# Weight sums moved into the quantisation loop, a deferred tail in the down projection, and a bf16 intermediate, in an eight-core two-layer transformer kernel

## The reference

```python
def _weight_quant(w):
    scale = 1.0 / jnp.clip(jnp.mean(jnp.abs(w)), 1e-05)
    return jnp.clip(jnp.round(w * scale), -1.0, 1.0) / scale
def _act_quant(x):
    scale = 127.0 / jnp.clip(jnp.max(jnp.abs(x), axis=-1, keepdims=True), 1e-05)
    return jnp.clip(jnp.round(x * scale), -128.0, 127.0) / scale
def _bitlinear(x, w):
    return jnp.einsum('bsi,oi->bso', _act_quant(x), _weight_quant(w))
gate = jax.nn.silu(_bitlinear(x, w_gate))      # w_gate, w_up: 4096 x 1024
up = _bitlinear(x, w_up)
out = _bitlinear(gate * up, w_down)            # w_down: 1024 x 4096
```

## Time and profile before

| | us |
|---|---|
| timed runs, median of 2 | 10397.83 (10381.49 to 10414.16) |
| the profiled execution, device time | 10226.14 |
| its span, slowest core (core 3) | 10224.6 |
| spans of the 8 cores | 10200.0 to 10224.6 |
| mean granted TensorE clock of the 8 cores | 0.623 to 0.624 of full speed |

### The profile page before, as it was taken

One profiled execution on the slowest core, in us unless ns is written; L12 is line 12 of the kernel. 1 busy time (PEld: TensorE's weight loads), 2 busy tenths in 40 slices (PEclk: granted clock), 3 DMA queues, 4 the chain that ended last, 5 costly groups with the idle time before them and its releaser, 6 DMA issues.

```text
span 10224.6 us, 48395 instructions; the slowest of 8 cores (10200.0 to 10224.6 us)
## 1 busy us (share of the span) xinstructions
PE 3471.7 (34%) x13683; PEld 1368.5 (13%) x13683; DVE 6251.7 (61%) x4796; ACT 1875.6 (18%) x2102; POOL 0.2 (0%) x4
## 2 busy tenths in 40 slices
PE   5766645999812111111011111000056531212112
PEld 2211112333301000000000000000023210101001
DVE  2555542222224999997899999966733325565565
ACT  0233311111111222222222222110121111111111
POOL 0000000000000000000000000000000000000000
PEclk9655557999955555555555565555578765555555
DMA  2000012111143332233323323234022221100100
GB/s 85 5 0 0 0 58 81 66 58 58 44 156 111 88 89 80 85 90 89 92 89 88 89 80 88 82 126 144 23 80 77 84 70 39 36 26 25 37 25 27
DMA packets 237113, 682.50 MB, mean 67 GB/s; under 512 B 31291, under 2 KB 64300, under 8 KB 230516
## 3 DMA queue, kind: packets, MB, share of 16 engines
q1 hardware_dynamic: 236852, 679.41, 21.3%
HBM read 599.36 MB, written 79.95 MB: 66 GB/s over the span
## 4 chain that ended last, share of the span: by engine, by line
DVE 48%; PE 26%; issue 10%; DMA 8%; ACT 6%; SPq 1%; DVEq 1%; ACTq 0%
DVE b_sl L1174 12%; DVE b_sl L1187 6%; DVE b_sl L1162 6%; DVE qd2B L1405 5%; PE p_hB L670 4%; PE p_eoB L701 4%; DVE ternB L1401 3%; PE p_dnB L1737 3%; PE p_gA L1556 2%; PE p_uA L1561 2%; DVE rb L443 2%; ACT attbuf L438 2%; DVE zbuf L432 2%; DVE qdD L1405 1%; DMA wstgB<-W 1%
## 5 line engine op out<-in xcount | busy, mean ns | idle before, releaser
L1174 DVE TENSOR_TENSOR_SCAN b_sl<-a_sl,h_state,b_sl 128x1024 f32<-128x1024 f32 x512 | 1175.7, 2338 | 43.7 <-ACT a_sl L1154 16.8
L1154 ACT ACTIVATE a_sl<-dt_ch,A_all 128x1024 f32<-128x1024 f32 x512 | 560.9, 1143 | 2291.5 <-DVE b_sl L1174 2266.3
L1224 PE MATMUL p_aoC<-wob,ybf 128*128 128x512 bf16 x512 | 166.8, 473 | 1867.9 <-DVE ybf L1209 1768.2
L1162 DVE TENSOR_TENSOR b_sl<-dxp_ch,bcb 128x2048 f32<-128x2048 f32 x256 | 585.1, 2285 | 67.0 <-DMA bcb<-bc_scr 65.6
L1187 DVE TENSOR_TENSOR b_sl<-b_sl,bcb 128x2048 f32<-128x2048 f32 x256 | 586.8, 2292 | 28.5 <-DVE h_state L1181 2.5
L1194 DVE TENSOR_TENSOR y_ch<-y_ch,b_sl 128x2048 f32<-128x2048 f32 x256 | 586.8, 2292 | 26.9 <-DVE b_sl L1187 0.5
L1719 PE MATMUL p_trB<-c_ident_bf,qbf2B 128*128 128x128 bf16 x512 | 74.9, 301 | 1368.0 <-DVE qbf2B L1707 1268.7
L432 DVE SCALAR_TENSOR_TENSOR zbuf<-c_alibi,p_z 128x1024 f32<-128x1024 f32 (+7 forms) x384 | 337.9, 908 | 306.7 <-PE p_z L415 161.0
L1083 PE MATMUL p_bigC<-x2Tc,wipz 128*128 128x512 bf16 x512 | 147.8, 460 | 1104.6 <-DMA wipz<-win_scr 1104.6
L701 PE MATMUL p_eoB<-w2b,hTe 128*128 128x512 bf16 x2048 | 501.3, 389 | 0.0
L1405 DVE SCALAR_TENSOR_TENSOR qd2B<-ternB,qd2B 128x2048 f32<-128x2048 f32 x192 | 440.1, 2292 | 20.0
(11 more groups left out here) (197 smaller groups left out, 5788.4 us busy)
## 6 DMA issues: line engine op xcount, KB each, us to landing
bcb<-bc_scr SPq DMA_DIRECT2D x512, 512.0 KB, 5.4
wstgB<-W SPq DMA_DIRECT2D x128, 512.0 KB, 4.3
gu_scr<-gubA SPq DMA_DIRECT2D x128, 256.0 KB, 2.0
guhB<-gu_scr SPq DMA_DIRECT2D x128, 256.0 KB, 3.6
wstgC<-W_in SPq DMA_DIRECT2D x16, 1024.0 KB, 7.3
x2r<-x_scr SPq DMA_DIRECT2D x32, 512.0 KB, 4.0
wipz<-win_scr SPq DMA_DIRECT2D x256, 64.0 KB, 5.7
wrowD<-w_gate SPq DMA_DIRECT2D x32, 512.0 KB, 3.8
```

Of the source, the lines that this page charges most:

```text
L1154: amk.append(s.emit("scalar", lambda h, j=j, dc=dc, s_=s_, d=dt2(qp): h.activation(out=a_sl[:, j * TC:(j + 1) * TC], in_=d[:, j * TC:(j + ...
L1162: bmk = s.emit("vector", lambda h, slot=slot, bs=bs: h.tensor_tensor(out=bs[:].rearrange("p (j t) -> p j t", t=TC), in0=dxp_ch[:].rearrang ...
L1174: scn.append(s.emit("vector", lambda h, j=j, dc=dc, s_=s_, bs=bs: h.tensor_tensor_scan(out=bs[:, j * TC:(j + 1) * TC], data0=a_sl[:, j * T ...
```

## The change

Three edits.

- The loop over the weight pieces becomes a generator, `d0_pieces`, that stops after each piece. The quantisation loop takes up to five pieces from it after each chunk, after the chunk's transposes. With 72 pieces this fills the chunks 0 to 13 and part of chunk 14. The means and thresholds are computed behind the quantisation loop. `wrow` and the quantisation's buffers now exist side by side.
- `gu_scr`, `gub` and `guh` are bf16 instead of f32. So a row maximum is taken over rounded values, and stores and reloads have half the bytes.
- In the down loop the tail (dequantisation, residual, layernorm, store) becomes a function. It is called for chunk t-1 at the end of the code of chunk t, and for the last chunk behind the loop.

The core of the diff:

```diff
-    gu_scr = nc.dram_tensor("gu_scr", [NT * 8 * 128, 512], F32, kind="Internal").ap()
+    gu_scr = nc.dram_tensor("gu_scr", [NT * 8 * 128, 512], BF16, kind="Internal").ap()
...
-        gub = SDa("gubA", [128, 2 * 512], F32)
+        gub = SDa("gubA", [128, 2 * 512], BF16)
...
-        guh = SDb("guhB", [128, 2048], F32)
+        guh = SDb("guhB", [128, 2048], BF16)
...
-        for wi, (tag, wsrc, npieces, wid) in enumerate(w_srcs):
-            acc_t = red_tok
-            for pc in range(npieces):
...
+        def d0_pieces():
+            red_tok = None
+            for wi, (tag, wsrc, npieces, wid) in enumerate(w_srcs):
+                acc_t = red_tok
+                for pc in range(npieces):
+                    r = pc % 2
+                    buf = wrow[:, r * 4096: r * 4096 + wid]
+                    s.wait("sync", ld_guard[r])
+                    ldw = dma("sync", buf, wsrc[pc], "wD%d" % r)
+                    s.wait("vector", ldw)
...
+                    yield
...
             tr_prev = s.token("tensor")
+            for _ in range(5):
+                if next(d0_gen, "end") == "end":
+                    break
         xqT_done = s.token("scalar")
         s.barrier()
         es_d2.close()
 
+        for _ in d0_gen:
+            pass
+        red_tok = red_tok_box[0]
...
+        pend_tail = None
         for tch in range(NT):
...
-            s.wait("vector", mt)
...
+            def dn_tail(tch=tch, par=par, mt=mt, ldx3b=ldx3b, pdn_=pdn_,
+                        outf_=outf_, x3c2_=x3c2_):
+                nonlocal prev_ln4
+                s.wait("vector", mt)
+                s.wait("vector", f2b)
+                s.wait("vector", prev_ln4)
...
+                vt4, st4 = layernorm(outf_, outf_, None)
+                prev_ln4 = st4
+                s.wait("sync", st4)
+                out_guards[par] = [dma("sync", out_t[tch], outf_, "outw%d" % par)]
+
+            if pend_tail is not None:
+                pend_tail()
+            pend_tail = dn_tail
+        pend_tail()
```

More of the change, by code:

```diff
@@ L1324, in build_program @@
                   ("d", w_down_h.rearrange("(a p) i -> a p i", p=128), 8, 4096)]
-        red_tok = None
+        red_tok_box = [None]
         ld_guard = [None, None]
-        for wi, (tag, wsrc, npieces, wid) in enumerate(w_srcs):
-            acc_t = red_tok
-            for pc in range(npieces):
[L1330 to L1376, removed]
@@ L1377, in build_program @@
-        wsc_done = mc_toks[-1]
-        s.barrier()
-        es_d0.close()
+        def d0_pieces():
[8 more added lines that the diff above has]
+                    s.wait("vector", ldw)
+                    s.wait("vector", acc_t)
+                    rt = s.emit("vector", lambda h, b=buf: h.tensor_reduce(
+                        out=wpart[:, 0:1], in_=b, axis=AXX, op=ALU.add,
+                        apply_absolute_value=True))
+                    ld_guard[r] = rt
+                    s.wait("vector", rt)
+                    if pc == 0:
+                        s.wait("vector", red_tok)
+                        acc_t = s.emit("vector", lambda h: h.tensor_copy(
+                            out=wpart[:, 1:2], in_=wpart[:, 0:1]))
+                    else:
+                        acc_t = s.emit("vector", lambda h: h.tensor_tensor(
+                            out=wpart[:, 1:2], in0=wpart[:, 1:2], in1=wpart[:, 0:1],
+                            op=ALU.add))
+                    yield
+                s.wait("tensor", acc_t)
+                s.wait("tensor", red_tok)
+                pt = s.emit("tensor", lambda h, wi=wi: h.matmul(
+                    out=p_d0[0:1, wi:wi + 1], lhsT=wpart[:, 1:2], rhs=onec,
+                    start=True, stop=True))
+                s.wait("scalar", pt)
+                red_tok = s.emit("scalar", lambda h, wi=wi: h.activation(
+                    out=totsb[0:1, wi:wi + 1], in_=p_d0[0:1, wi:wi + 1], func=AF.Copy))
+                red_tok_box[0] = red_tok
@@ L1381, in ternary @@
+        d0_gen = d0_pieces()
         def ternary(dst_ap, src_ap, wi, dep_toks):
@@ L1745, in build_program @@
             ldx3b = dma("sync", x3c2_, x3_scr_t[tch], "x3b%d" % par)
[L1746 to L1765 removed]
+            def dn_tail(tch=tch, par=par, mt=mt, ldx3b=ldx3b, pdn_=pdn_,
[4 more added lines that the diff above has]
+                s.wait("vector", prev_ln4)
+                for g_ in out_guards[par]:
+                    s.wait("vector", g_); s.wait("scalar", g_)
+                dq = s.emit("vector", lambda h: h.tensor_scalar(
+                    out=outf_, in0=pdn_, scalar1=f2_all[:, tch:tch + 1], scalar2=None,
+                    op0=ALU.mult))
+                dn_guard[par] = dq
+                s.wait("vector", ldx3b)
+                s.wait("vector", dq)
+                radd = s.emit("vector", lambda h: h.tensor_tensor(
+                    out=outf_, in0=outf_, in1=x3c2_, op=ALU.add))
+                x3ld2_g[par] = radd
+                s.wait("scalar", radd)
+                s.wait("vector", radd)
+                vt4, st4 = layernorm(outf_, outf_, None)
[6 more added lines that the diff above has]
+        pend_tail()
         s.barrier()
```

29 lines of the change are left out of this document (23 added, 6 removed).

## The result

The changed kernel takes 9954.85 us (median of 11 runs, 9852.85 to 10057.77), the kernel before, run beside it, 10354.24 (10 runs). The ratio is 0.963, with a 95% interval of 0.958 to 0.969: 3.7% faster, where 3.5% were forecast (9868 / 10226.1 = 0.965). It leaves out runs in which the cores of one die were clearly slower than the others; the medians over all runs give 0.961. The absolute forecast, 10037, is 82 us above the median, and the median lies 10 us under the low end of the stated range (9965); the direction and the size of the change came as forecast, the base did not.

The account below looks back on a forecast made before the run. No engine fills the span (VectorE 61%, TensorE 34%), so waits decide. Savings of 302 + 40 + 16 = 358 us from 10226.1 give 9868; scaled 10034 or subtracted 10040, the forecast is 10037 us, range 9965 to 10110.

Parts of the forecast that it names:

- The deferred tail: Down loop: matmuls hidden beside the next chunk's ladder, 88.1 us per chunk in place of 107.6; about 302 us saved.
- (a): Down loop: square doesn't wait for evictions, so the whole matmul and transpose wait vanishes; 482 us saved, 9908 us; chance 0.03.
- (b): Tail hides its matmuls, but moved pieces and halved rows lose 37 and 31 us; 234 saved, 10160 us; chance 0.06.
- (c): Down loop: the tail's waits bind it to its own chunk's matmuls; only 56 us saved, 10341 us; chance 0.02.
- The pieces: Quantisation loop: weight sums moved in remove only waits, for loads and for ScalarE; 40 us saved.
- the loss at the activation loads: Quantisation loop: each activation load is issued behind five piece loads on SyncE; 6 us lost in all.
- bf16: Down loop: halved reloads shorten the path by 1.1 us in each of 15 reloads; 16 us saved, ends -31 and +31.
- the 1.5 of the rows: Down loop: 1.5 us saved per reload by 0.52 MB less, if bytes decide.
- the 1.1 of the cut: Down loop: the 1.5 us per reload cut to 1.1 for the smaller rows; 16 us over 15 reloads.
- (d): Gate/up: TensorE's clock stays at 1.2 GHz throughout, costing 403 us; slower than before, 10444 us; chance 0.02.
- The factor 1.0168: Whole kernel: median of two timed runs, 10397.8 us, over the profiled 10226.1; used to scale the forecast time.

Follow-up runs that it names:

- the run with the square ahead: Full change, but the tail of chunk t-1 is written ahead of the transposes and evictions of chunk t; ratio 0.954 to the kernel before, down 1337.3 us.
- bf16 only: Kernel before with only the three buffers in bf16; one profiled execution, down 1697.6 us against 1725.4, gate/up 848.5 us.

## Why the prediction was right

- **The deferred tail** (forecast 302 us): 298.7 alone. Each step of the sum is in the timeline: evictions' end 11.9 us behind the ladder (8862.81 against 8850.92), the tail 3.7 us from the square's start to its end (3.8 forecast), the matmuls covered, the chunk 15 uncovered (13.6 us, 12 forecast), the wait of 9 us for the square. The period came to 86.6 us and not 88.1, of which 1.1 to 1.4 is the reload that I had booked separately.
- **The rival with the whole wait gone** (a) fell in the way that was argued, by ScalarE's queue; the run with the square ahead showed it.
- **The rivals (b) and (c)** did not come: the pieces gained 50 us, bf16 gained too, and only one activation load is waited for, 3.1 us; and the matmul wait of (c) is left once, 13.6 us, not 16 times.
- **The pieces** (forecast 40 us): 50. The waits for pieces fell by 30.6 us (22 + 8 forecast) and ScalarE's by 13.5 (13 forecast). The step that was mis-sized is the loss at the activation loads, 6 us in the sum: it was nothing, since SyncE issues that load (6841.04) 5 us ahead of its use, and two reductions and two waits lie between. With that the term is 46; of the last 4 us, 2.3 are VectorE's busy time on core 3 (405.5 to 403.2), and the rest is not split further.
- **bf16** (forecast 16 us, from a cut of 1.5 to 1.1 us per reload): 21.7 on top of the tail, 1.4 per reload; alone, the wait for the reload fell by 1.3 per chunk in the mean of the cores and by 1.1 on core 3. So bytes decided for the most part, and what was measured lies between the 1.5 of the rows and the 1.1 of the cut.
- **Slower by the clock** (d): gate/up took 849.2 us at 0.77, and in its first burst the clock reads 1.00 from 7405 us on. The rival did not come.
- **The base.** The factor 1.0168 between the profiled execution and two timed runs was taken for a property of the kernel. With ten runs the kernel before has a median of 10354 and runs down to 10229, and the profiled executions of all ten kernels have cores that reach the first DMA of the feed-forward anywhere from 6784 to 6981 us, in code that no kernel changed. The slowest core is late by as much as it meets of that. The ratio was the number to forecast. Of the 82 us by which the time was too high, 44 are the base (10398 against 10354) and 13 are missing in the sum; the other 26 show in no stage of the feed-forward in the profiled executions, and their cause is open. The lowest runs of the two kernels, 10229 and 9853, lie 376 us apart, near the sum of the stages.

Added up on the means: 298.7 + 50.3 + 21.7 = 370.7 us in the feed-forward's stages, against 358.

## What to carry to other kernels

When a wait is taken off the busiest engine, write down what the next engine has in its queue ahead of the thing now waited for: here 17 us of matmul time were hidden, and 9 of the 28 us stayed because eight evictions stood ahead of one square. An order by hand is best read queue by queue, and the fix is to put long-lead work (a load, the pass that needs it) ahead of a long stretch of the busy engine, not behind it. Work that only fills, like weight sums, should be spread over that stretch at the distance of a load's latency; here five in a row left 70 us of waits and one at a time none.

## What the runs showed of the hardware

- VectorE, between dependent steps, has a gap of 0.1 to 0.2 us that an independent instruction fills. The merged first stage, which I took to have a floor of some 450 us on core 3 (541.8 less the waits of 70.2 and 21.5), ran in 441.8.
- Halving the bytes of a reload at the same number of packets cut its time nearly in step with the bytes: the engines' share over 7 us went from 63.3 to 45.4%, with rows of 1 KB in place of 2 KB beside an unchanged store, and the median from issue to landing on core 3 from 3.6 to 2.6 us.
- The down burst of the kernel before begins at a granted clock of 0.50 (1.2 GHz), after 79.8 us in which TensorE only waited and then the 32 transposes, and reads 1.00 (2.4 GHz) from 8807 us on, 6.5 us after its start; the one shown of bf16 only reads 1.00 from 2.7 us after its start. On core 3 most bursts of 64 take 15.3 to 16.9 us. The exposed waits for them came to 451.2 to 455.2 us per core in one execution and 442.2 to 447.5 in another; with the tail deferred they are covered and the down stage of the full change differs by 1.5 us between the cores.
